# Sums over edges in a graph network: the weight moved into the one-hot matrices, products summed in PSUM per node tile, loops written out

## The reference

```python
edge_index = jnp.stack([src, dst])
x = _layernorm(x + _L0_gnn_ref(...))   # graph attention, 4 heads, batch norm
x = _layernorm(x + _L1_gnn_ref(...))   # two GCN convolutions, 512 -> 256 -> 512
x = _layernorm(x + _L2_gnn_ref(...))   # GraphSAGE
x = _layernorm(x + _L3_gnn_ref(...))   # one convolution, sums by src
...
# GCN convolution, twice; self loops included in src, dst and w
norm = dinv[src] * w * dinv[dst]
out = jax.ops.segment_sum(h[src] * norm[:, None], dst, num_segments=n_nodes) + b
# GraphSAGE
msg = x[row] * edge_weight[:, None]
x_neigh = jax.ops.segment_sum(msg, col, num_segments=n_nodes)
# the last layer: dst, src = edge_index[0], edge_index[1]
output = jax.ops.segment_sum(support[src] * edge_vals[:, None], dst, num_segments=input.shape[0])
```

## Time and profile before

| what | value |
|---|---|
| timed runs | 4093.15, 4099.45, 4100.37 us; median 4099.45 |
| profiled execution, its span (the time that it has) | 4580.2 us, 63,826 instructions |
| busy in it: PE, PEld | 3028.5 us (66%), 1656.8 us (36%) |
| DVE, ACT, POOL | 2534.5 us (55%), 1784.3 us (39%), 2891.1 us (63%) |
| stages on the time axis of the profile (us) | g1 1692 to 2280, gcn_hidden to 2300, g2 to 2900, gcn_output to 3095, g3 to 3690, sage_output 3692 to 3904, g4 3915 to 4516, conv_output to 4580 |

### The profile page before, as it was taken

How to read it: one execution, slowest core, us unless ns; L and a number is a source line. 1 busy time by engine, 2 the same in 40 slices (tenths; PEclk the granted TensorE clock), 3 DMA queues, 4 the chain that set the end, 5 groups by cost and what they waited for, 6 DMA issues and landing times. The chain is left out here.

```text
span 4580.2 us, 63826 instructions
## 1 busy us (share of the span) xinstructions
PE 3028.5 (66%) x11605; PEld 1656.8 (36%) x11606; DVE 2534.5 (55%) x4864; ACT 1784.3 (39%) x3995; POOL 2891.1 (63%) x3191
## 2 busy tenths in 40 slices
PE   7566665377677665655545556686777799577773
PEld 6344443244444243333323333342222244222221
DVE  8455554666666663434433444574555654565656
ACT  3111111366666563333323333334444433344444
POOL 5666666666666666666666666676666667566662
PEclk8777776688999886667656666798999999899997
DMA  3211111355555153323243332335666611566653
GB/s 101 74 45 63 48 60 39 116 168 163 162 162 162 47 154 88 87 87 89 86 137 87 88 88 86 72 72 171 175 172 174 173 50 42 143 173 176 174 170 124
DMA packets 207412, 520.84 MB, mean 114 GB/s; under 512 B 63334, under 2 KB 70638, under 8 KB 206892
## 3 DMA queue, kind: packets, MB, share of 16 engines
q0 software_dynamic: 157600, 413.73, 31.9%
q1 hardware_dynamic: 49714, 105.90, 7.5%
HBM read 475.94 MB, written 43.49 MB: 113 GB/s over the span
## 5 line engine op out<-in xcount | busy, mean ns | idle before, releaser
L1639 PE MATMUL g_part<-g_rows,g_hot 128*128 x3328 | 1549.2, 614 | 864.7 <-ACT g_rows L1560 499.7
L1615 DVE TENSOR_TENSOR k_acc<-k_acc,g_part 128x256 f32 (+1 forms) x1664 | 920.5, 553 | 1073.0 <-PE g_part L1639 350.2
L1639 PEld LDWEIGHTS g_part<-g_rows,g_hot 128*128 128x128 f32 x3328 | 749.4, 243 | 1664.4 <-issue 1596.2
L1560 ACT ACTIVATE g_rows<-g_rows,k_rec 128x256 f32<-128x256 f32 (+1 forms) x1176 | 663.8, 577 | 1096.6 <-PE g_part L1639 255.0
L1223 POOL DMA_INDIRECT at_rows<-h_table,at_index x392 | 390.9, 997 | 249.7 <-ACTq L1249 132.5
L1285 PE MATMUL at_part<-at_rows,at_hot 128*128 x832 | 401.0, 567 | 187.8 <-DVE at_hot_first L1299 68.9
L1580 POOL DMA_INDIRECT g_rows<-support,g_index x392 | 379.3, 968 | 220.6 <-issue 120.7
L1580 POOL DMA_INDIRECT g_rows<-x_scaled_w,g_index x392 | 383.3, 978 | 212.3 <-issue 121.8
L1580 POOL DMA_INDIRECT g_rows<-hidden_scaled,g_index x392 | 380.7, 971 | 214.6 <-issue 139.6
L1580 POOL DMA_INDIRECT g_rows<-x,g_index x392 | 380.3, 970 | 210.3 <-issue 112.9
L673 POOL DMA_INDIRECT edges_by_dst<-fr_records,f_dst_slots x392 | 384.1, 980 | 167.6 <-issue 166.8
(11 more groups left out here) (409 smaller groups left out, 3705.1 us busy)
## 6 DMA issues: line engine op xcount, KB each, us to landing
f_rows<-low_rows SPq DMA_DIRECT2D x28, 896.0 KB
x<-n_out SPq DMA_DIRECT2D x50, 256.0 KB
f_x_in<-in_x SPq DMA_DIRECT2D x25, 256.0 KB
h_table<-f_h SPq DMA_DIRECT2D x25, 256.0 KB
gat_h_all<-h_table SPq DMA_DIRECT2D x5, 1280.0 KB
n_x<-in_x SPq DMA_DIRECT2D x25, 256.0 KB
n_x<-x SPq DMA_DIRECT2D x25, 256.0 KB
support<-k_acc SPq DMA_DIRECT2D x25, 256.0 KB
```

The lines of the kernel that those rows point to most:

```text
L1560: act.activation(rows[:, n, :], rows[:, n, :], ACT.Copy, scale=col(rec[:, :, R_W], g * BT + (h * BT + n))).then_inc(weighed, 1)
L1615: dve.tensor_tensor(here, here, part[u % RING][:, 0:width].unsqueeze(1), ALU.add).then_inc(added, 1)
L1639: pe.matmul(part[u % RING][:, 0:width], hot[:, u % (2 * HOTS), :], rows[:, bass.ds(place[n], 1), :].rearrange("p o f -> p (o f)"), start=T ...
```

## The change

The change applies to `aggregate` and what it needs. What it does, engine by engine:

- **VectorE** compares and multiplies in one instruction per pair (`is_equal`, then `mult` with the weight), so a one-hot matrix holds the weight itself. There are 16 such matrices in a ring (8 in g4) in place of 8. VectorE adds no product any more, and loads no registers.
- **TensorE** adds up the products in PSUM (`start=False`), in the bank of the pair's node tile modulo 4 (`BANKS`). At the start of a stage it writes four products of a blank row into the banks; it loads a third set of registers, the node tile, and waits for `opened` ahead of each product. It gives the 16 counts only when the banks have been opened.
- **ScalarE** opens each bank, with the tile's earlier content of `acc` (g1, g2) or with zeros (g3, g4, `keep=False`), and copies it to `acc` when the last product of the tile is in. That point is a new row of the table, `T_ENDS`, made by two more small products in `PairTable.sums`. It doesn't weigh rows and makes no index copies.
- **SyncE** takes over the release of row slots from ScalarE, with the register loads of `T_DONE`.
- **GpSimd** issues the same 392 gathers, with the index read from the records themselves.
- All programs but TensorE's are straight, with no loop. The weights are spread to pairs, as the local numbers are: by a fourth channel in `attention_weights` and by four products in `Records`. g4's clearing of `acc` and ScalarE's clearing in `gcn_output` are gone.

In the diff the old body of `aggregate`, which stands above, is left out.

```diff
+BANKS, T_ENDS = 4, TILES_PAD
...
+        ends = self.banks[2][0:1, EC:EC + NT]
+        pe.matmul(ends, self.w.pair[:, 0, self.here], self.k.ident[0:NT, 0:NT], start=True, stop=False, skip_group_check=True)
+        pe.matmul(ends, self.k.ones[0:1, 0:1], self.k.columns[0:1, 2 * BT:2 * BT + 1].broadcast_to([1, NT]),
+                  start=False, stop=True, skip_group_check=True).then_inc(self.summed, 1)
...
-        act.wait_ge(self.summed, 3)
+        act.wait_ge(self.summed, 4)
+        act.copy(self.table[0:1, T_ENDS:T_ENDS + NT], self.banks[2][0:1, EC:EC + NT])
...
-        SEEN = 3
+        SEEN = 4
...
+                spread(3, zt[:, :, R_W], False)
...
-                evict(1, own_att, HEADS)
-                act.copy(tiles(rec[:, 0:EC, :], R_W), turned_rows(1)).then_inc(evicted_act, 1)
+                evict(1, own_att, HEADS).then_inc(evicted_act, 1)
                 act.wait_ge(turned, 3)
                 act.copy(rec[:, 0:TILES, R_LOCAL], p_t[2][:, 0:TILES]).then_inc(evicted_act, 1)
+                act.wait_ge(turned, 4)
+                act.copy(rec[:, 0:TILES, R_W], p_t[3][:, 0:TILES]).then_inc(evicted_act, 1)
...
-        for field, bank in ((R_OTHER, self.p_row), (R_W, self.p_weight)):
-            for i in range(SPAN // P):
-                last = pe.transpose(bank[:, i * ROWS_T:(i + 1) * ROWS_T], self.zt[:, i * P:(i + 1) * P, field], ident)
-            last.then_inc(self.turned, 1)
+        for i in range(SPAN // P):
+            last = pe.transpose(self.p_row[:, i * ROWS_T:(i + 1) * ROWS_T], self.zt[:, i * P:(i + 1) * P, R_OTHER], ident)
+        last.then_inc(self.turned, 1)
         pe.wait_ge(self.chosen, 1)
+        for i in range(SPAN // P):
+            last = pe.matmul(self.p_weight[:, 0:TILES], self.zt[:, i * P:(i + 1) * P, R_W], self.sel[:, i, :],
+                             start=(i == 0), stop=(i == SPAN // P - 1))
+        last.then_inc(self.turned, 1)
...
-        act.copy(self.rec[:, 0:EC, R_W].rearrange("p (r i) -> p i r", i=SPAN // P), self.tiles(self.p_weight))
+        act.copy(self.rec[:, 0:TILES, R_W], self.p_weight[:, 0:TILES])
...
+def aggregate(nc, k, name, rec, pairs, table, width, acc, fetch=(), source=None, keep=True):
+    RING = 16 if source is None else 8
     with Scope(nc, name) as s:
         rows = s.sb("rows", [P, BT, width])
+        hot = s.sb("hot", [P, RING, P])
+        blank = s.sb("blank", [1, F])
+        part = s.ctx.enter_context(nc.psum_tensor(f"{name}_part", [P, BANKS, F], FP))
         gathered = [s.sem(f"gathered{n}") for n in range(BT)]
+        arrived, freed = s.sem("arrived"), s.sem("freed")
+        hot_ready, summed = s.sem("hot_ready"), s.sem("summed")
+        blank_made, blanked, opened_first, opened, evicted = (
+            s.sem(n) for n in ("blank_made", "blanked", "opened_first", "opened", "evicted"))
         fetched = s.sem("fetched")
...
+                held = [sp.alloc_register(f"{s.name}_done{n}") for n in range(BT)]
+                sp.sem_inc(freed, BT - LAG)
+                for e in range(EC):
+                    n = e % BT
+                    if n == 0:
+                        done = at_least_one(sp, held, registers(nc, mybir.EngineType.SP, pairs, T_DONE, e, 1,
+                                                                TILES + 2 * BT))
+                    sp.wait_ge(gathered[n], (e // BT + 1) * 16)
+                    sp.sem_inc(arrived, 1)
+                    sp.wait_ge(summed, done[n])
+                    sp.sem_inc(freed, 1)
+            @block.gpsimd
+            def _(pool):
+                if records is not None:
+                    records.fill(pool)
+                    pool.wait_ge(records.rowed, 1)
+                for e in range(EC):
+                    pool.wait_ge(freed, e + 1)
+                    pool.indirect_dma_start(rows[:, e % BT, :], None, table,
+                                            bass.IndirectOffsetOnAxis(other[:, e, R_ROW:R_ROW + 1], 0)).then_inc(gathered[e % BT], 16)
...
+                zero = k.ones[:, 0:1].broadcast_to([P, width])
+                def open_bank(t):
+                    here = part[:, t % BANKS, 0:width]
+                    begin = act.copy(here, acc[:, t, 0:width]) if keep else act.activation(here, zero, ACT.Copy, scale=0.0)
+                    begin.then_inc(opened if t else opened_first, 1)
+                held = [act.alloc_register(f"{s.name}_ends{n}") for n in range(BT)]
+                act.wait_ge(blanked, 1)
+                for t in range(BANKS):
+                    open_bank(t)
+                for t in range(NT):
+                    n = t % BT
+                    if n == 0:
+                        ends = at_least_one(act, held, registers(nc, mybir.EngineType.Activation, pairs, 0, T_ENDS + t, 1,
+                                                                 TILES + 2 * BT, min(BT, NT - t)))
+                    if t:
+                        act.wait_ge(opened, t)
+                    act.wait_ge(summed, ends[n])
+                    act.copy(acc[:, t, 0:width], part[:, t % BANKS, 0:width]).then_inc(evicted, 1)
+                    if t + BANKS < NT:
+                        act.wait_ge(evicted, t + 1)
+                        open_bank(t + BANKS)
+                act.wait_ge(evicted, NT)
+                act.sem_inc(opened, 1)
...
+                dve.memset(blank[:, :], 0.0).then_inc(blank_made, 1)
...
-                    dve.memset(acc[:, :, 0:width], 0.0).then_inc(cleared, 1)
...
+                for j in range(TILES):
+                    if j >= RING and j % 4 == 0:
+                        dve.wait_ge(summed, 2 * BT + j - RING + 4)
+                    dve.tensor_scalar(hot[:, j % RING, :], k.columns[:, 0:P], rec[:, j, R_LOCAL:R_LOCAL + 1],
+                                      rec[:, j, R_W:R_W + 1], ALU.is_equal, ALU.mult).then_inc(hot_ready, 1)
...
+                pe.wait_ge(blank_made, 1)
+                for b in range(BANKS):
+                    last = pe.matmul(part[:, b, :], k.ones[0:1, :], blank[:, :], start=True, stop=True, skip_group_check=True)
+                last.then_inc(blanked, 1)
+                pe.wait_ge(opened_first, 1)
+                pe.wait_ge(opened, BANKS - 1)
                 pe.sem_inc(summed, 2 * BT)
                 held = [pe.alloc_register(f"{s.name}_need{n}") for n in range(BT // 2)]
+                turn = [pe.alloc_register(f"{s.name}_turn{n}") for n in range(BT)]
                 with pe.Fori(0, TILES // BT // 2) as i:
                     g = i * 2
                     for h in range(2):
+                        at = g * BT + h * BT
+                        place = registers(nc, mybir.EngineType.PE, pairs, T_PLACE, at, 0, BT - 1)
+                        need = at_least_one(pe, held, registers(nc, mybir.EngineType.PE, pairs, T_NEED, at, 1, EC)[1::2])
+                        tile = node_tiles(nc, mybir.EngineType.PE, pairs, at)
+                        at_least_one(pe, turn, tile)
                         for n in range(BT):
                             u = h * BT + n
+                            if n % 4 == 0:
+                                pe.wait_ge(hot_ready, g * BT + (u + 4))
                             if n % 2 == 0:
+                                pe.wait_ge(arrived, need[n // 2])
+                            pe.wait_ge(opened, turn[n])
+                            pe.matmul(part[:, bass.ds(tile[n] % BANKS, 1), 0:width].rearrange("p o f -> p (o f)"), hot[:, u % RING, :],
                                       rows[:, bass.ds(place[n], 1), :].rearrange("p o f -> p (o f)"),
+                                      start=False, stop=True, skip_group_check=True).then_inc(summed, 1)
...
-            act.activation(a[:, q, :].unsqueeze(1), acc[:, bass.ds(t, 1), 0:HID], ACT.Copy,
-                           scale=col(w.dinv, t)).then_inc(taken, 1)
-            act.wait_ge(taken, t + 1)
-            act.sem_inc(passed, 1)
-            return act.activation(acc[:, bass.ds(t, 1), 0:F], k.ones[:, 0:1].unsqueeze(2).broadcast_to([P, 1, F]), ACT.Copy,
-                                  scale=0.0)
+            return act.activation(a[:, q, :].unsqueeze(1), acc[:, bass.ds(t, 1), 0:HID], ACT.Copy,
+                                  scale=col(w.dinv, t))
...
-            aggregate(nc, k, "g3", rec, dst_pairs, x2, F, acc)
+            aggregate(nc, k, "g3", rec, dst_pairs, x2, F, acc, keep=False)
...
+                aggregate(nc, k, "g4", rec_src, src_pairs, support, F, acc, source=by_src, keep=False)
```

More of the change, by code:

```diff
@@ L122, in col, with registers @@
     return ap[:, bass.ds(j, n)]
-def registers(nc, engine, table, row, j, low, high):
+def registers(nc, engine, table, row, j, low, high, n=BT):
     _, values = nc.values_load_multi_w_load_instructions(
-        table[row:row + 1, bass.ds(j, BT)], engines=[engine], min_val=low, max_val=high,
+        table[row:row + 1, bass.ds(j, n)], engines=[engine], min_val=low, max_val=high,
```

(14 more changed lines are left out.)

76 lines of the change are left out of this document (8 added, 68 removed).

## The result

The changed kernel takes 4061.14 us (median of 4 runs, 4059.28 to 4065.52) against 4099.57 us for the kernel before: ratio 0.991, interval 0.9896 to 0.9924. In two later groups of runs the kernel before took 4093.7 and 4106.6 us, and the changed one 0.9911 of the latter (4070.38 us). On one further chip the kernel before took 4502.09 us; its runs are compared only with each other.

What follows compares the result with a forecast made beforehand. The prediction took GpSimd's 392 gathers a stage, at a 1.25 us floor, as the pace, with most recorded stalls absent from timed runs. Its terms, -40 - 10 + 9 + 7 - 9 = -43, gave 4056 us; 8-in-10 range 3890 to 4170.

Steps and rivals of the forecast that it cites:

- The floor of a gather: GpSimd's gathers in g1 to g4: 1.25 us from start to start, before and after, 490 us a stage.
- the recording: Stalls in g1 to g4: 388 us over the gathers' floor, read as sequencers held up by the profiling itself.
- the gap of 480.8 us: Whole kernel: profiled span 4580.2 us against timed median 4099.45, taken as support that timed runs lack the stalls.
- the first rival: Gathers of g1 to g4: the recorded stalls are real and half of 388 us goes, 3902 us; chance 0.20.
- The split of the 50 us: Loop of g1 to g4: -40 us from dropping adds and weighing, -10 from fewer compares lengthening gathers.
- The rival of the compares: GpSimd's descriptor work: single compares delay gathers, 58 us a stage, 4288 us; chance 0.14.
- The opening: Start of g1 to g3: fifth gather 9.3 us in instead of 6.7, +9 us in all.
- release of a slot, cost 0: Row slots in the gather loop: SyncE releases them instead of ScalarE, free because GpSimd runs 4 gathers ahead.
- The ends: End of each stage: two products and one copy replace the last adds, -2.2 us x 4 = -9.
- Elsewhere 0: Outside g1 to g4: gcn_output's dropped zeroing and attention_weights' fourth channel, run while TensorE waits for scans, change nothing.
- The rival of the openings: Stages g1 to g4: no loop gain left; openings, ends and collisions cancel, 4099 us, no change; chance 0.16.
- The rivals of the sequencer and of SyncE: g1 to g4: TensorE's sequencer becomes the bound, 4176 us, chance 0.08; SyncE releases slots later, 4212 us, chance 0.04.

Runs made afterwards that it cites:

- run 11: The changed kernel, unchanged, run again beside the kernel before: 4070.38 us, ratio 0.9911.
- experiment 8: The kernel before with loops written out and four single compares without the weight for each four-wide one, on the slow chip: 4486.11 us, ratio 0.9963.
- experiments 5 and 6: The changed kernel on the slow chip: first with every compare of g1 to g3 made twice, 4446.98 us; then with the weights' copy behind ScalarE's zeroing, 4435.75 us.
- experiment 2: The kernel before with only the loops of GpSimd, ScalarE and VectorE in g1 to g4 written out: 4093.14 us, ratio 0.9997.
- run 12: The kernel before with loops written out and four single compares without the weight for each four-wide one, beside the changed kernel: 4073.66 us, ratio 0.992.
- experiments 3, 4 and 11: The changed kernel with TensorE's counts ahead of the opening, 4057.83 us; also with register loads ahead of the wait for opened banks, 4049.83 us; and unchanged, 4070.38 us.

## Why the prediction was right, and which steps were not

4056 us was forecast, 4061 measured. The direction and the place (392 gathers at their floor, so that little is to be gained) were right; that the number came so close is in part luck, since the largest term was not worked out from a cause. By the two clean profiles (the kernel before recorded again, and the changed one), with the ninth gather's start taken from the timelines:

| term | forecast | measured |
|---|---|---|
| steady loop and compares, ninth to last gather | -40 - 10 | 1980.2 to 1929.9: -50.3 |
| openings of g1 to g3, start to ninth gather | +9 | +2.8, +1.9, +4.2 |
| opening of g4 | +7 | +4.4 |
| ends, last gather to the last add or product | -9 | 25.3 to 23.2: -2.1 |
| attention weights | 0 | +1.6 (+6.9 with run 11 for the changed kernel) |

The terms add up to -37.5 us. The two executions' spans differ by 30.9; parts that the change doesn't touch took the other 6.6 us more in the second.

- **The floor of a gather** held: 1.25 us from start to start, and the changed kernel's four stages need 1929.9 us for 1532 of them, 15 us above 1532 x 1.25. That the timed runs held few of the recorded stalls held too (62 of 388 us). Its reason, the recording, was wrong: a recorded execution of the same kernel takes what a timed one does, and the pauses come with the chip. The inference from the sum of stalls and the gap of 480.8 us was sound; the mechanism was not shown by it. On the slow chip the first rival's stalls are real, and part of them goes: 138 pauses in experiment 8 stand against 89 and 87 in experiments 5 and 6.
- **The split of the 50 us** failed. I gave the collisions of compares and gathers 10 us and the loop without weighing and adds 40. The 40 was the 39 us that a sum across two conditions left over; the clean profile's span is 1.7 us below its own time, so launch explains none of it, and that 40 + 10 meets 50.3 is luck. The collisions are 30.5 to 37.7 us of gather time (1523.4 or 1530.5 less 1492.8), and undoing them alone shortened the stages from first to last gather by 25 to 31 us (2025.2 in experiment 2 or 2031.2 to 2000.4) and the time by 33. The rest of the change's loop gives the remainder: run 12's ninth to last gathers take 1949.6 us and run 11's 1926.6, 23 us less. Weighing, adds and the moved release were not taken apart. Against that stand run 11's openings (+14.6) and attention weights (+7.5) and its ends (-2.6): -3.5 us for all of the change but its compares, and 3.3 measured. The step at fault was that I scaled the new compare from the front's scatters and kept 7 us a stage for it (36 less 28 was then taken as 10): it adds about 1 us a stage on average, the mean being 949 to 954 ns with it and the median 949. Its own time was off too, 0.34 us for 0.28, which cost nothing.
- **The rival of the compares** (0.14) fell: twice as many in three stages cost 7 to 9 us. The Trainium skill's "SBUF — State Buffer", section Who interferes with whom, has tensor_scalar in a two-port mode block GpSimd fully, and tensor_tensor contend only with its reads; here the tensor_tensor was the dearer. The longest gather is 1468 ns beside the tensor_tensor form of two SBUF inputs and 1048 beside single tensor_scalar compares in run 12. The trace so bears out that two SBUF inputs contend, which the prediction passed over as the lesser case. The single compares did not hold up descriptor work as a full block would; whether they ran in such a mode no row tells.
- **The opening** came as worked out: the fifth gather of g1 9.4 us after the start, 9.3 forecast, with two errors that cancel (the blank products took 7.2 us and not 5.9, the copies 1.3 and not up to 2.5). In g2 the step "release of a slot, cost 0" failed: I named the last wait on the fetches but not that SyncE's first release stands behind eight fetch DMAs. The sum hardly shows it (+1.9 for a forecast of +3), because the early gathers of g2 had been slow beside those same fetches before.
- **The ends** failed: the last copy into `acc` does come sooner (18.4 us behind the last gathers in sum, against 25.3 for the last adds), but the padding pairs belong to a tile past the last one, whose `opened` ScalarE gives only after every eviction, and their product ends 1.0 us behind the copy in g1 and g2 and 1.4 in g3 and g4. That gives 4.8 of the 6.9 us back. In the changed kernel's timeline of g3 the last product waits for it:

```profile
3264.78 0.59 ACT L1598 COPY k_acc<-g_part 128x512 f32<-128x512 f32 x1 [2.85 <-PE g_part L1647]
3265.70 1.10 PE L1647 MATMUL g_part<-g_rows,g_hot 128*128 x2 [1.01 <-ACTq L1603]
```

- **"Elsewhere 0"** failed by the attention weights: I looked at TensorE's idle time and not at what ScalarE has queued behind its new wait. The cost is 1.6 us in one execution and some 7 in three (experiments 3, 4 and 11), where the granted clock was 0.50 there.
- **The rival of the openings** fell: they cost 13 us against the 50 gained in the loop. **The rivals of the sequencer and of SyncE** fell: from the ninth to the last gather the changed kernel needs less than run 12 (1926.6 against 1949.6 us).

## What to carry to other kernels

Where GpSimd's gathers set the pace, look at the longest and the mean of them beside the median: 1.5 us against 0.95 was here the mark of an engine beside it, of VectorE's compares with both inputs in SBUF and not of its adds, and four small tensor_scalar compares in place of one wide tensor_tensor cost VectorE more time (1.12 us against 0.69) and the kernel 33 us less. A step moved to another engine stands behind what that engine issues first (fetches, a zeroing), and that has to be counted as closely as its own cost. Before stalls of a profile are argued about, compare its span with the timed runs; if they differ by a tenth, record the kernel again.

## What the hardware showed that was not expected

The same program took 4094 us on one chip and 4502 us on another, with gathers' rows 3.5 us late about every 20 us on the second and register instructions of up to 0.7 us; the change gained more there, since two kernels within some 3 us of it took 0.985 to 0.986 of the time before. In both profiles of the kernel before, gathers were lengthened beside VectorE's compares of two SBUF inputs (up to 1468 ns) and not beside its adds of an SBUF and a PSUM input (at most 963 ns).
